# One graph-attention layer pair on one core: an early one-hot moved to the other engine, one small product moved behind three others, and the last store cut in two

## The reference

```
def gat_layer(x, W, a_s, a_d, b, edge_index, concat):
    h = (x @ W).reshape(n, H, C)
    alpha_s = einsum('nhc,hc->nh', h, a_s);  alpha_d = einsum('nhc,hc->nh', h, a_d)
    e = leaky_relu(alpha_s[src] + alpha_d[dst], 0.2)
    e = exp(e - segment_max(e, dst)[dst])
    alpha = e / (segment_sum(e, dst)[dst] + 1e-16)
    out = segment_sum(h[src] * alpha[:, :, None], dst)
    return out.reshape(n, H * C) + b
h = elu(gat_layer(x, W1, ...))            # 8 heads of 768 features
out = gat_layer(h, W2, ...)               # 1 head of 768 features
return layernorm(x + out)                 # rows of 768, 512 of them
```

## Time and profile before

| | us |
|---|---|
| median of 3 runs | 637.04 (636.98 to 637.24) |
| profiled execution, its own time | 636.94 |
| its span | 635.0 |

### The profile page before, as it was taken

The page is one execution under the profiler, slowest core; times in us unless marked ns, Lnnn a source line. Parts: engine busy times, 40 slices in busy tenths (PEclk is TensorE's granted clock), DMA queues, the critical chain, the costliest instruction groups (busy, mean ns, idle before and its releaser), DMA issues.

```text
span 635.0 us, 9251 instructions
## 1 busy us (share of the span) xinstructions
PE 626.7 (99%) x3353; PEld 536.9 (85%) x3362; DVE 536.8 (85%) x974; ACT 337.6 (53%) x570; POOL 210.6 (33%) x133
## 2 busy tenths in 40 slices
PE   9999999999999999999999999999999999999996
PEld 5766568989888898989899988999898989887885
DVE  8999997989989887778686958797798869898967
ACT  7899992545625645553354635363445344534282
POOL 2000000131643834076405840384208540451230
PEclk9999999999999999999999999999999999999999
DMA  8422403116153423043302520260217130500002
GB/s 321 161 71 81 148 27 100 50 51 199 34 166 122 153 98 102 1 141 109 100 0 71 179 65 11 76 224 19 81 40 233 52 100 6 218 26 0 1 2 99
DMA packets 22172, 59.34 MB, mean 93 GB/s; under 512 B 2544, under 2 KB 2800, under 8 KB 22128
## 3 DMA queue, kind: packets, MB, share of 16 engines
q1 hardware_dynamic: 21984, 58.69, 28.0%
q10 hardware_dynamic: 144, 0.07, 0.0%
HBM read 54.03 MB, written 4.72 MB: 93 GB/s over the span
## 4 chain that ended last, share of the span: by engine, by line
PE 85%; DVE 10%; issue 1%; ACT 1%; DMA 1%; POOL 1%; ACTq 0%; DVEq 0%
PE O L1390 27%; PE R L1281 8%; PE R L1287 8%; PE R L1284 8%; PE O L1298 7%; PE R L1357 6%; PE R L1363 6%; PE R L1360 6%; DVE ohd L728 1%; DVE L L885 1%; PE O L1357 1%; PE O L1363 1%; PE O L1360 1%; PE O L1539 1%; PE O L1545 1%
## 5 line engine op out<-in xcount | busy, mean ns | idle before, releaser
L1195 POOL TENSOR_TENSOR W2l<-Wr,W2h 128x768 fp32r<-128x768 f32 x48 | 91.9, 1935 | 133.3 <-ACT W2h L443 133.3
L1281 PE MATMUL R<-W1h,xTh 128*128 128x384 f32 x312 | 106.1, 340 | 0.4 <-ACT h L455 0.4
L1199 POOL TENSOR_TENSOR Pl<-L,Ph 128x512 fp32r<-128x512 f32 x34 | 55.9, 1662 | 152.4 <-ACT Ph L491 152.4
L1287 PE MATMUL R<-W1h,xTl 128*128 128x384 f32 x312 | 104.8, 336 | 0.0
L1284 PE MATMUL R<-W1l,xTh 128*128 128x384 f32 x312 | 104.8, 336 | 0.0
L1189 POOL TENSOR_TENSOR W1l<-Wr,W1h 128x768 fp32r<-128x768 f32 x30 | 59.6, 2010 | 116.9 <-ACT W1h L432 116.8
L768 DVE CUSTOM_DVE_ANT_0 junk<-h,abc 128x768 bf16<-128x768 f32 x64 | 66.9, 1046 | 23.2 <-ACT h L455 21.6
L1390 PE MATMUL O<-W2h,gh 128*128 128x256 f32 (+1 forms) x384 | 78.2, 338 | 0.0
L1390 PE MATMUL O<-W2h,gl 128*128 128x256 f32 (+1 forms) x384 | 77.8, 337 | 0.0
L1390 PE MATMUL O<-W2l,gh 128*128 128x256 f32 (+1 forms) x384 | 77.2, 335 | 0.0
L1357 PE MATMUL R<-Ph,hh 128*128 128x512 f32 x168 | 66.3, 395 | 0.0
(11 more groups left out here) (201 smaller groups left out, 1178.3 us busy)
## 6 DMA issues: line engine op xcount, KB each, us to landing
Wr<-in_W SPq DMA_DIRECT2D x101, 384.0 KB, 3.6
abc<-in_as SPq DMA_DIRECT2D x9, 384.0 KB, 4.1
abc<-in_ad SPq DMA_DIRECT2D x9, 384.0 KB, 5.3
h_rows<-h SPq DMA_DIRECT2D x8, 384.0 KB, 2.3
hl<-h_rows SPq DMA_DIRECT2D x8, 384.0 KB, 5.9
xin<-in_xT SPq DMA_DIRECT2D x6, 256.0 KB, 5.7
xr<-in_x SPq DMA_DIRECT2D x1, 1536.0 KB, 7.7
out<-res SPq DMA_DIRECT2D x4, 384.0 KB, 2.3
```

Of the source, the lines that this page charges most:

```text
L1195: e.tensor_tensor(W2l[:, m % N2, :], Wr[:, n, :], W2h[:, m % N2, :].bitcast(f32), ALU.subtract).then_inc(s_w2l, 1)
L1199: e.tensor_tensor(Pl[:, t, d0:d1], L[:, t, d0:d1], Ph[:, t, d0:d1].bitcast(f32), ALU.subtract).then_inc(s_Pl, 1)
L1281: e.matmul(bank[:, 0:HALF], xTh[:, f, xs], hi[:, ws], start=f == 0, stop=False)
L1287: m = e.matmul(bank[:, 0:HALF], xTl[:, f, xs], hi[:, ws], start=False, stop=f == FT - 1)
```

## The change

Three edits. First, ScalarE's single early `ohs` is that of block 2 and no longer of block 1; VectorE makes the one of block 1. Second, in the last head's `stage_C` the product `columns` comes behind the three products of group 1's first chunk and no longer ahead of them. Third, VectorE scales the last tile in two instructions, 512 and 256 columns wide, and two transfers store it: SP issues the first 512 columns (256 KB) and ScalarE the other 256 (128 KB), each behind its own piece. The wait for all stores, on SP, counts one more.

```
     def on_act(j):
-        return j == 1 or j >= 14 and j % 16 in (1, 3, 5, 8, 10, 12, 14)
+        return j == 2 or j >= 14 and j % 16 in (1, 3, 5, 8, 10, 12, 14)
...
                 if d < NT - 1:
                     e.wait_ge(s_rs, 2 * d + 2)
+                    e.dma_start(outv[:, d, :], res[:, d, :]).then_inc(s_out, 16)
                 else:
                     e.wait_ge(s_fin, 1)
-                e.dma_start(outv[:, d, :], res[:, d, :]).then_inc(s_out, 16)
-            e.wait_ge(s_out, 16 * NT)
+                    e.dma_start(outv[:, d, 0:512], res[:, d, 0:512]).then_inc(s_out, 16)
+
+            e.wait_ge(s_out, 16 * NT + 16)
...
+            e.wait_ge(s_fin, 2)
+            e.dma_start(outv[:, NT - 1, 512:768], res[:, NT - 1, 512:768]).then_inc(s_out, 16)
...
-                    e.tensor_scalar(
-                        res[:, d, :], res[:, d, :], mv[:, d, 0:1], rs[:, d, 1:2], ALU.subtract, ALU.mult).then_inc(s_fin, 1)
+                    for lo, hi in ((0, 512), (512, 768)):
+                        e.tensor_scalar(
+                            res[:, d, lo:hi], res[:, d, lo:hi], mv[:, d, 0:1], rs[:, d, 1:2], ALU.subtract, ALU.mult).then_inc(s_fin, 1)
...
             for n in range(6):
                 for c in range(LASTC, FT):
                     stage_C(H - 1, c, groups=(n,))
-                if n == 0:
-                    columns(H, take("x", H, 0))
+                    if n == 1 and c == LASTC:
+                        columns(H, take("x", H, 0))
```

## The result

The changed kernel is slower, by a little less than the 0.2% that the prediction had counted as no change:

| | before | after |
|---|---|---|
| median | 637.16 us (636.93 to 637.45, 16 runs) | 638.36 us (638.16 to 638.53, 16 runs) |
| profiled execution, own time | 636.94 | 638.36 |
| its span | 635.0 | 636.5 |

The account below looks back on a forecast made before the run. With PE busy 99% of the span, only TensorE's waits and the stretch after its last product could move the time. One-hot 0, columns +0.12, last tile -0.15 gave -0.03 us; forecast 636.95 us, range 636.5 to 637.3.

Parts of the forecast that it names:

- the last tile's: End of the kernel: two pieces and two stores end the bytes at 633.93 instead of 634.10; taken as -0.15 us.
- the one-hot: Start: block 1 goes at about 4.9, but the 0.40 us come back as a wait for W1l; value 0.
- the columns: Around 601 us: 0.39 us of wait saved, rm's rows 0.32 later, TensorE then waits at L1553; +0.12 us.
- the pieces: VectorE's last tile: pieces of 0.51 and 0.34 us, overlapping by 0.08, end 0.09 us later than the whole.
- what lies behind the last issue: End: from the second store's issue at 632.37, its bytes run behind the first's until 633.93; -0.26 us.
- The 7.35: Start: L1409, at 7.75 before, would start near 7.35 because block 1 moves 0.40 us into idle time.
- Rival C: Columns' 0.32 us arrive whole at L1553 and dn: 637.2 us, or 637.36 without the store's gain; chance 0.15.
- Rival A: End: the last store's 128 KB land by their own size, -0.58, the rest +0.12: 636.6 us; chance 0.20.
- Rival B: Start, columns and end: the waits come back in full, -0.40, -0.39 and -0.15: 636.1 us; chance 0.03.
- Rival D: Wait at 601 us was not for rm, so moving columns changes nothing: 636.9 us; shares the forecast's 0.60.

Follow-up runs that it names:

- g_extra_end: Kernel before with one small memset of an unused column as VectorE's very last instruction: 638.13 against 637.20 us, ratio 1.0014.
- g_eight: Kernel before with eight small VectorE memsets between its last sum y2 and the denominators, 14 us ahead of the end: 636.99 against 637.20 us, ratio 0.9999.
- g_after_eight: Changed kernel with eight small VectorE memsets between y2 and the denominators: 637.11 us against 637.20 of the kernel before, ratio 0.9999.
- g_after_moved: Changed kernel with the VectorE instruction that makes sel given to GpSimd: 636.98 us against 637.31 of the kernel before, ratio 0.9997.
- e_onehot: Kernel before with the first edit alone, ScalarE's early one-hot being that of block 2: 637.31 against 637.26 us, ratio 1.0001.
- e_columns: Kernel before with the second edit alone, columns behind the three products of group 1: 637.32 against 637.26 us, ratio 1.0001.
- g_split_sp_moved: Kernel before with the last tile in two pieces, both stored by SP, and sel made by GpSimd: 636.86 against 637.31 us, ratio 0.9994.
- e_store: Kernel before with the third edit alone, last tile in two pieces stored by SP and ScalarE: 638.10 against 637.26 us, ratio 1.0013.
- e_small_alone: Kernel before with the last tile scaled in two pieces but only columns 512 to 767 stored, by SP: 636.79 us in one execution.
- e_one_store: Kernel before with the last tile scaled in two pieces, stored whole by SP behind the second: 638.30 against 637.34 us, ratio 1.0016.
- g_extra: Kernel before with one small VectorE memset of an unused column in the third head: 637.39 against 637.31 us, ratio 1.0002.
- e_row_halves: Kernel before with the last tile scaled whole, stored by SP in two transfers of 64 rows: 638.41 against 637.34 us, ratio 1.0019.
- e_small_first: Kernel before with the last tile scaled and stored by SP in two pieces, 256 columns first, then 512: 638.12 against 637.34 us, ratio 1.0014.
- g_best: Kernel before, last tile in two pieces stored by SP, sel made by GpSimd, columns behind one product: 636.69 against 637.20 us, ratio 0.9992.

## Why the prediction was wrong

**The step that failed is the last tile's**, and in it something left out. I priced the split by VectorE's time, the issue and the bytes, -0.15 us, and gave +0.16 as its worst. Most of the bytes were not far from the forecast: two issues 0.33 us apart (forecast 0.26), the first bytes 0.83 us after the first issue (0.82), and all but the last data packet through 1.81 us after the second (1.56). That last packet came 0.35 us behind the rest, and the landing 1.0 us behind it instead of 0.35. I had taken what lies between the bulk of the bytes and the landing to be a constant. One more instruction of VectorE brings a fetch of instructions from 1 us behind the span's end to beside the last store, and the store then lands 1.0 us later. `g_extra_end` shows the cause without the split (+0.93 us), `g_eight`, `g_after_eight` and `g_after_moved` take it away again. The count was there, 974 instructions of VectorE before and 975 with the second piece, but I looked only at what the instruction does; where a longer list would put the fetch, no row of before told.

In the sum, against what the trace shows: the one-hot 0 (measured: nothing, `e_onehot`), the columns +0.12 (+0.20 in this trace, +0.13 to +0.19 in `e_columns`), the pieces +0.09 (+0.20: the pair took 0.87 us where one took 0.68; the pieces took 0.55 and 0.41, not the 0.51 and 0.34 of my line), what lies behind the last issue -0.26 (+0.80 instead). Without the fetch, in `g_split_sp_moved`, that last term comes true: from the second issue to the end of the span are 635.0 - 632.61 = 2.39 us, -0.33 against before. With ScalarE as the issuer, in `g_after_moved`, they are 635.68 - 633.22 = 2.46, -0.26.

**The one-hot.** Value right. My picture was half right: the load still comes 0.12 us after `W1l`, but L1409 didn't start 0.40 us sooner, nor block 1 at 4.9. TensorE's granted clock is given as 1.00 in this stretch in every trace, but the products tell its level: 512 columns 0.43 us apart are its lower one (1.2 GHz), 0.22 apart its upper (2.4 GHz). Before, it had warm-up products every 0.43 us and then went at 0.22 from block 0 on; in the changed kernel block 0 still went at 0.43, and the pace of 0.22 starts at 5.37. Where it starts differs between executions whatever the edit (with the old one-hots, the 0.43 lasts to 6.7 in `e_store`), and in the traces of `e_onehot` and `e_store`, where TensorE reached L1409 only at 8.73 and 8.58, it was TensorE that came last, 0.7 to 1.0 us behind `W1l`. The 7.35 was out of reach even at the upper level: VectorE ends the `ohs` of block 6 at 7.13 here and at 6.98 before, and the block's two products take 0.43, so that about 7.5 (an estimate from these) was the soonest. So the value is 0 by the trace of the changed kernel, but the step that gave 7.35 was wrong.

**The columns.** The delay of 0.32 us and the wait that returns were as forecast, with 0.21 us left of them. Two details were not. TensorE met the delay first at 613.86, 0.61 us ahead of a load, for ScalarE's copy of the second small bank; I had only named L1553. And the 0.08 us that a product behind a wait was to give back did not come: +0.20, not +0.12. Rival C had the place and a sixth of the loss. Rival A needed the small store to land about 1.6 us after its issue (bytes through at 633.52); undelayed, as the second of two, it took 2.0 to 2.1. Rival B falls with TensorE's wait at 613.86. Rival D falls too: the wait at 601 is gone, and the first `L` row came 0.32 us later.

**The chances.** I left 0.02 for anything outside my cases, because no row paid for more. Each case was a sum of durations that the trace shows; none allowed for a resource that the rows show only by its count, the fetch queue.

The Trainium skill (DMA: Bandwidth & Descriptors, "Queues, rings and completion order") states that a transfer's semaphore write lands only after every earlier write of the same DMA engine, across its queues. The runs fit that: where the fetch moved at 633.7 to 634.8, while the store was in flight, the store landed about 1.0 us late; where it moved behind the store's last packet (`e_small_alone`, 634.04 against 634.03) or 3 us sooner (`g_eight`) it didn't.

The traces of the late stores show more. A store reports its landing by sixteen counts. In all seven late ones fifteen come in time and the last 0.9 to 1.1 us behind them: in the changed kernel by 635.04 and at 636.14. In `g_after_eight` the last comes 0.02 us behind the fifteenth (634.88), in `e_small_alone` 0.22. And in all seven a data packet of the store starts as the fetch's ends, within 0.01 us: 635.09 here, 635.00 in `e_one_store`, 634.01 in `g_extra`. So the delay sits in one sixteenth of the store, and begins with a packet that waits for the fetch. That both are on one DMA engine is my reading; the trace names no engine. Why the last count then takes 1.0 us from its packet, where it takes 0.35 undelayed, no run here shows.

## What to carry to other kernels

When a change adds an instruction to an engine, even one that nobody waits for, look in the profile at where the instruction queues' packets lie, above all around the last store: here one memset at the very end cost 0.93 us, and eight of them 14 us earlier cost nothing that the runs could show. If an edit to the tail costs more than its rows, first compare the count of instruction packets, then shift the list by a few instructions before judging the edit. A product moved out of a wait gives only what the chain behind its result can spare: ask which wait is next for both sides, and move it by one step, not by three.

## What the runs showed of the hardware that I had not expected

- A queue of instruction fetches, which shifts when VectorE's list grows, stands among the DMA queues: 17 packets of some 8 KB in the span before, 18 after. One that falls beside the last store holds back a data packet of it by about 0.4 us and its landing from 2.3 to 3.3 us (`g_extra_end`, `e_one_store`, `g_extra`).
- TensorE's step from 0.43 to 0.22 us per product of 512 columns came at 4.5 us in one execution and at 7.1 in another (before, `e_onehot`), behind the same warm-up products, while the profile gives the granted clock as 1.00 throughout.
- Stores of 64 rows of 3 KB kept the DMA engines 91% busy at 197 GB/s (`e_row_halves`, 634 to 635 us), about half the rate of 128 rows (390 GB/s at 96%), though rows of 2 KB and 1 KB from 128 partitions moved at 280 to 430 GB/s in slices of 0.2 us (after).
- A 128 KB store that no fetch delays lands 1.7 to 2.1 us after its issue (`e_small_first`, `e_small_alone`, `g_best`, `g_after_eight`), a 384 KB store 2.3: two thirds fewer bytes save 0.2 to 0.6 us.
